# First attention: VectorE's part of the projections and of the output projections, two tiles behind TensorE's part

## What is computed

```python
h = (x - mu) * rsqrt(var + 1e-05) * ln_gamma + ln_beta
qkv = (h @ w_qkv + b_qkv).reshape(B, T, 3, NUM_HEADS, HEAD_DIM)
q, k, v = ...
scores = einsum('bhqd,bhkd->bhqk', q, k) / sqrt(HEAD_DIM)
attn = softmax(scores, axis=-1)
out = einsum('bhqk,bhkd->bhqd', attn, v)
out = out.reshape(B, T, C) @ w_out + b_out
return residual + out
```

## Time and profile before

| | us |
|---|---|
| median of 3 runs | 2835.35 (2833.18 to 2835.89) |
| profiled execution, its own time | 2833.97 |
| its span in the trace | 2832.2 |
| busy in the span: PE | 2683.1 (95%) |
| PEld | 1990.9 (70%) |
| DVE | 2418.7 (85%) |
| ACT | 2024.1 (71%) |
| POOL | 1482.4 (52%) |

### The profile page before, as it was taken

How to read it: one execution, slowest core, us unless ns; L and a number is a source line. 1 busy time by engine, 2 the same in 40 slices (tenths; PEclk the granted TensorE clock), 3 DMA queues, 4 the chain that set the end, 5 groups by cost and what they waited for, 6 DMA issues and landing times.

```text
span 2832.2 us, 45753 instructions
## 1 busy us (share of the span) xinstructions
PE 2683.1 (95%) x16263; PEld 1990.9 (70%) x16263; DVE 2418.7 (85%) x4394; ACT 2024.1 (71%) x4477; POOL 1482.4 (52%) x1076
## 2 busy tenths in 40 slices
PE   6999999999999999999999999999999999999996
PEld 3333333333367777888888888888888888898895
DVE  7999999899768887788888888888978988988886
ACT  2887877778765555777777777777777777777773
POOL 2311302100045555666677667677667776766763
PEclk7999999999999999999999999999999999999997
DMA  4121021210022210000000000000000000000000
GB/s 131 37 67 37 28 81 37 66 37 17 2 79 89 88 61 6 3 1 1 1 1 3 3 1 3 3 1 3 3 1 3 3 1 3 3 1 3 3 3 6
DMA packets 41316, 65.18 MB, mean 23 GB/s; under 512 B 5176, under 2 KB 15992, under 8 KB 41088
## 3 DMA queue, kind: packets, MB, share of 16 engines
q1 hardware_dynamic: 41088, 62.26, 6.8%
HBM read 45.86 MB, written 15.86 MB: 22 GB/s over the span
## 4 chain that ended last, share of the span: by engine, by line
PE 56%; DVE 30%; issue 6%; ACT 5%; POOL 2%; DMA 0%; SPq 0%; DVEq 0%; ACTq 0%; POOLq 0%
PE P L1845 16%; PE P L1870 9%; DVE a_mx L1238 8%; DVE c_nm L1404 6%; PE P L1707 6%; PE P L1856 5%; PE P L1774 4%; DVE c_DT L1429 4%; PE P L1669 4%; PE P L1879 3%; PE P L1681 3%; PE P L1785 2%; ACT a_PT L801 2%; PE P L1828 2%; DVE c_Tl L1437 1%
## 5 line engine op out<-in xcount | busy, mean ns | idle before, releaser
L1404 DVE TENSOR_REDUCE c_nm<-P 128x1 f32<-128x1024 f32 x512 | 622.1, 1215 | 107.2 <-PE P L1845 105.7
L930 ACT ACTIVATE c_P<-P,c_nm 128x1024 f32<-128x1024 f32 x512 | 571.9, 1117 | 181.2 <-DVE c_nm L1404 180.5
L1238 DVE TENSOR_REDUCE a_mx<-P 128x1 f32<-128x512 f32 x1024 | 634.2, 682 | 33.5 <-PE P L1669 29.6
L2068 POOL TENSOR_TENSOR c_P<-c_P,c_P 128x1024 f32<-128x1024 f32 (+1 forms) x256 | 617.3, 2411 | 21.3
L801 ACT ACTIVATE a_PT<-P 128x512 f32<-128x512 f32 x976 | 509.0, 603 | 128.7 <-PE P L1681 127.1
L2066 POOL TENSOR_SCALAR c_P<-c_P,c_rr 128x1024 f32<-128x1024 f32 (+1 forms) x256 | 296.0, 1156 | 444.1 <-DVE c_rr L1416 444.0
L1870 PE MATMUL P<-c_DT,c_xkh 128*128 128x256 f32 x2048 | 390.1, 284 | 2.7 <-DVE c_DT L1429 2.7
L1845 PE MATMUL P<-c_xth,c_Th 128*128 128x512 f32 x1024 | 365.9, 438 | 18.1 <-ACT c_P L930 18.1
L1429 DVE TENSOR_TENSOR c_DT<-P,c_DT 128x512 fp32r<-128x512 f32 x512 | 348.3, 680 | 9.3 <-ACT c_DT L941 8.8
L1681 PE MATMUL P<-a_Qs,a_Ks 32*128 32x512 f32 x976 | 319.8, 482 | 32.8 <-ACT a_PT L801 26.4
L1870 PEld LDWEIGHTS P<-c_DT,c_xkh 128*128 128x128 f32 x2048 | 327.9, 192 | 5.7 <-DVE c_DT L1429 5.7
(11 more groups left out here) (245 smaller groups left out, 5143.2 us busy)
## 6 DMA issues: line engine op xcount, KB each, us to landing
b_cwB<-cw_scratch SPq DMA_DIRECT2D x64, 256.0 KB, 5.0
qk_scratch<-a_nh SPq DMA_DIRECT2D x32, 256.0 KB, 3.4
a_Ks<-qk_scratch SPq DMA_DIRECT2D x32, 256.0 KB, 2.9
a_Qs<-qk_scratch SPq DMA_DIRECT2D x32, 256.0 KB, 3.7
c_stg<-in_cw SPq DMA_DIRECT2D x8, 640.0 KB, 3.9
qk_scratch<-a_nl SPq DMA_DIRECT2D x16, 256.0 KB, 3.5
b_stg<-in_moe SPq DMA_DIRECT2D x9, 384.0 KB, 3.2
out<-xres SPq DMA_DIRECT2D x15, 128.0 KB, 1.8
```

What stands on the lines that cost most here:

```text
L930: e.activation(m.P1[s][n % 4][:, :], P[:, k:k + 2, :].rearrange("p c k -> p (c k)"), ACT.Exp, bias=m.nm[:, n % 4, s:s + 1], accum_out=m.sm ...
L1238: e.tensor_reduce(m.mx2[u % 2][:, t // 4, j, t % 4, half:half + 1], bank("maxima", u, t, j, half), AX, ALU.max).then_inc(m.S["a_max_dve"])
L1404: e.tensor_reduce(m.nm[:, n % 4, s:s + 1], P[:, k:k + 2, :].rearrange("p c k -> p (c k)"), AX, ALU.max, negate=True).then_inc(m.S["c_nm"])
L2068: e.tensor_tensor(p0, p0, p1, ALU.add).then_inc(m.S["c_D"])
```

## The change

The two steps are cut in two. `project` and `out_project` keep TensorE's and ScalarE's part; VectorE's part becomes a step of its own, `project_low` and `out_add`, that follows in the plan two ticks behind, one tick for the last batch's output projections. The tables of signals and of bank releases are changed to match, and batch 0's projections are followed by their low part at once.

```diff
 FOLLOWS = {
+    "project": lambda b, wh, c: [(2, ("project_low", b, wh, c))] if b else [],
+    "out_project": lambda b, r: [(1 if b == B - 1 else 2, ("out_add", b, r))],
     "row2": lambda u, c: [(2, ("row2_low", u, c))],
...
-    "project": {"a_qk_pe": 1, "a_nh": 1, "a_nl": 1},
+    "project": {"a_qk_pe": 1, "a_nh": 1},
+    "project_low": {"a_nl": 1},
...
-    "out_project": {"a_op_pe": 1, "a_add": 1},
+    "out_project": {"a_op_pe": 1},
+    "out_add": {"a_add": 1},
...
-    "project": lambda *a: [("a_nl", "project", *a)],
+    "project": lambda *a: [("a_nl", "project_low", *a)],
...
-    "out_project": lambda *a: [("a_add", "out_project", *a)],
+    "out_project": lambda *a: [("a_add", "out_add", *a)],
...
             put(("project", 0, wh, c))
+            p.do("project_low", 0, wh, c)
             p.do("keep_heads", 0, wh, c)
...
-    def project(b, wh, c):
+    def project_low(b, wh, c):
         cs = slice(512 * c, 512 * c + 512)
         w.wait_ge(*at("a_nh", "project", b, wh, c))
...
-    def out_project(b, r):
+    def out_add(b, r):
```

More of the change, by code:

```diff
@@ L1181, in ln_stats @@
         elif who == "x1":
-            w.wait_ge(*at("a_add", "out_project", b, 1))
+            w.wait_ge(*at("a_add", "out_add", b, 1))
         else:
@@ L1610, in vector_engine @@
     parts = dict(first=first, first_hn=first_hn, ln_stats=ln_stats, ln_gather=ln_gather, ln_apply=ln_apply,
-                 turn_h=turn_h, values=values, project=project, maxima=maxima, row1=row1,
-                 divide=divide, out_project=out_project, m_turn_x=m_turn_x,
+                 turn_h=turn_h, values=values, project_low=project_low, maxima=maxima, row1=row1,
+                 divide=divide, out_add=out_add, m_turn_x=m_turn_x,
                  route=route, route_turn=route_turn, choose_step=choose_step, product=product, halves=halves, finish=finish, small=small,
@@ L2133, in keep_heads @@
                 S[f"a_qk{c}"], 16)
-        w.wait_ge(*at("a_nl", "project", b, wh, c))
+        w.wait_ge(*at("a_nl", "project_low", b, wh, c))
         e.dma_start(m.qk[wh, :, 2 if wh else 1, :, cs], m.nl[wh][:, cs].bitcast(F32)).then_inc(S[f"a_qk{c}"], 16)
```

## The result

| | before | after |
|---|---|---|
| median of the runs, us | 2835.2 (2833.18 to 2835.89, 4 runs) | 2851.48 (2849.07 to 2908.23, 4 runs) |
| profiled execution, its span | 2832.2 | 2847.2 |
| mean granted clock of TensorE | 0.985 | 0.983 |

The changed kernel is slower: ratio 1.0055, 95% interval 1.0028 to 1.0082. The run of 2908.23, 2% longer than the other three at a lower granted clock (0.954), is not in the ratio. The spans differ by 15.0 us.

A forecast was written before the change was run, and what follows sets the result against it. The prediction took a closed loop of TensorE and ScalarE's exponent as the bound, with VectorE outside it. Pairs' 6.1 us plus output projections' 4.1, summed as 10.3, on the median of 2835.35 gave 2845.6 us, 0.36% slower, range 2839 to 2851.

The forecast's parts named there:

- What bounds the loop: First attention's regular groups: a closed loop of TensorE and ScalarE's exponent, 2.63 us; VectorE outside it with 0.15 us spare.
- The stalls stay: VectorE's wait at projection pairs: not removed but lengthened, 1.33 + 0.40 us, now ahead of the next tile's reduction.
- Projections, 6 x 1.02: Six projection pairs: low part and the scores matmuls behind it each 1.02 us later, 6.1 us in all.
- Output projections, 6 x 0.69: Six output projections: addition 1.04 us later, 0.35 covered by the exponent's wait, 0.69 paid each, 4.1 us in all.
- Making up: Groups behind a moved step: nothing given back in the sum; VectorE's 0.15 us spare per group only in the lower bound.
- The sum: Whole kernel: 6.1 + 4.1 = 10.3 us added to the median of 2835.35, giving 2845.6 us.
- (c): Around projection pairs: longer TensorE idle brings more clock falls, up to 1.7 us each, 2847 to 2854 us; chance 20%.
- (a): First attention: VectorE is the true bound and the removed stalls return 11.5 us, 2823.9 us; chance 6%.
- (b): Around the moved steps: nothing moves, VectorE's later start is absorbed by existing waits, 2835 to 2840 us; chance 11% within 0.2%.

The follow-up runs named there:

- after_filled: The changed kernel with five useless TensorE matmuls in the idle time ahead of the second scores matmul behind each pair; ratio 1.0031 to the kernel before.
- low_only: Against the kernel before, only the projections' low parts moved behind the next reduction, output projections' additions left in place; ratio 1.0066.
- after_again: The changed kernel run once more, unaltered, to see how much its clock falls vary; ratio 1.0116 to the kernel before.
- before_filled: The kernel before with two useless TensorE matmuls in its idle time at each of six pairs; ratio 1.0001.
- before_again: The kernel before run once more, unaltered, as a single run without a ratio; first pairs took 4.65, 4.63 and 4.66 us.
- add_only: Against the kernel before, only the output projections' additions moved, low parts left in place; ratio 1.0024.
- split_behind: Against the kernel before, each pair's second half projected one tile later and each low part put one reduction later; ratio 1.0002.
- low_filled: Against the kernel before, only the low parts moved, with five useless TensorE matmuls in the idle time at each pair; ratio 1.0025.
- three_ticks: The changed kernel with low parts and additions three ticks behind instead of two, so two reductions stand ahead; ratio 1.0262 to the kernel before.

## Why the prediction was right, and where its size was off

- *What bounds the loop.* Right. Groups with nothing special stayed at 2.63 to 2.64 us in every kernel wherever the clock was at its upper level, and took 4.09 at the lower; with VectorE's work unchanged, only the waits for banks and the clock moved the time.
- *The stalls stay.* Right: VectorE's idle ahead of the moved work rose from 1.33 to 1.74 us (1.73 forecast) and moved to the reduction.
- *Projections, 6 x 1.02.* Measured 0.97 in the three first pairs; in the second ones 1.75, 1.01 and 1.05, falls of the clock included. In after_filled, where the clock didn't fall, it is 0.94 to 0.98 in all six. The low part was 0.05 us sooner behind the reduction than forecast (spacing 0.60, 0.54 behind the matmul, 0.80 to the scores).
- *Output projections, 6 x 0.69.* Measured 0.66 in each of six, 4.0 us instead of 4.1.
- *Making up.* Two later groups gave back 0.25 us each (3.21 became 2.96); I had taken none.
- *The sum.* The steps are 5.8 + 4.0 - 0.5 = 9.3 us, where I had 10.3. The profiled executions differ by 15.0. The missing 5.7 is in the main rival (c), the clock: in batch 1 the second pair and the two groups behind it take 4.3 us more than with the filler (7.40, 5.33, 3.80 against 6.63, 2.95, 2.64), in batch 2 1.5 more; batch 3 has 1.5 in both kernels. 4.3 + 1.5 = 5.8, and 9.3 + 5.8 = 15.1.
- *Luck in that closing.* Two more differences cancel. The five groups of sums near the loop's end take 14.45 us before (750.76 to 765.21) and 16.71 after (765.57 to 782.28), and what follows the loop's last sums takes 2048.1 us before and 2046.1 after. Neither goes with the change: the five groups take 13.7 to 16.7 us and the rest 2044.1 to 2049.6 in the profiles of all these kernels. The clock in the two stretches, before and then after:

```profile
750.00:770.00 20.00, 17.51 (x111) 5.85 (x111) 9.38 (x25) 14.25 (x20) 1.87 (x2) 0.91 0.01 2
```

```profile
765.00:785.00 20.00, 17.69 (x93) 5.05 (x94) 8.89 (x22) 12.16 (x17) 1.69 (x2) 0.74 0.00 1
```

- *Where the size was off.* The term left at nothing in the likeliest case, "the clock falls as well", which I gave 20% and priced at 1.7 us a fall. It was the rule, not the exception: after and low_only have falls behind all three second pairs in the profiled execution, where before had one. A short one costs 1.5 us, near the price given, but a long one 4.3. The direction and the steps were right and the total was short by it: 0.36% forecast, 0.55% measured. The median of 2851.48 us is 0.5 us above the top of the range of 2839 to 2851; the ratio, taken on the 2835.35 that I started from, gives 2850.9. That it came no higher is partly luck: the same kernel, run once more as after_again, took 2854.3 to 2901.4 us.
- *The rivals (a) and (b)* are out: no group with a moved part was shorter or unchanged.

What stays open is why the falls are longer in one set of runs than in another, and whether before's own falls can be prevented: before_filled shows none at its pairs in its profiled execution, but its interval (0.9965 to 1.0037) tells nothing. Open too is why the loop begins at the lower level of the clock in some executions: until 72 us in before_again, 107 in add_only and split_behind, 182 in after_again, 218 in low_filled. That costs up to some 54 us in one execution, far more than the change, and a run without a trace may hold some of it.

## What to carry to other kernels

Before putting ready work ahead of a waiting instruction, check two things in the order of time: is that work really ready sooner (here its matmul stood behind the very projection that was waited for), and is anyone waiting for the instruction that is moved back. The second is one view of the waits: if the bound engine appears there as waiting for it, the delay is paid, less what another wait in the same place covers (here 0.97 of 1.01 us were paid at a pair, 0.66 of 1.04 at an output projection). And price an idle time of TensorE by what the clock does after it, not by its length alone: two waits of 1.43 us, 8 us apart, cost up to 4.3 us more behind them, and a few useless matmuls in the gap won them back.

## What the runs showed of the hardware

TensorE's granted clock was 1.00 in 200 to 300 us of the kernel before, where it was busy for 92.95 us of the 100. It fell to the lower level (1.2 GHz; the sums row took 1.94 us instead of 1.06, a regular group 4.09 instead of 2.63) after idle times of 1.43 us in two pairs 8 us apart, in all three batches of the profiled executions of after and low_only. With idle times of 2.02 us its mean was 0.83 over 155 us in three_ticks. It stayed at 1.00 through the same waits for the low parts with 1.41 us of matmuls in them. A long idle time is not the only thing that goes before a fall: before had one behind a pair with a wait of 0.44 us, in one batch of three, and in batch 3 of split_behind the clock was down already at the first wait for a low part, of 0.59 us (the scores matmul behind it took 0.79 us instead of 0.49).

The Trainium skill, page "TensorE: Matmul & The Clock Gate", section "A second HAM failure mode: psum-queue depth-cycling", says that where TensorE goes round PSUM banks and is idle for a short time between groups of matmuls often enough, its clock swings between the two levels; the trace agrees (0.77 and 0.72 behind the second pair), and the filled kernels show it by their difference. Unexpected was the size: the profiled execution of three_ticks was 50.6 us longer than before's, of which 17 us are its steps, so the clock cost an estimated 34 us on top; by the ratio of the runs it would be 57.
